# Attention turns in pairs of tiles: one burst of weighted sums for two tiles, small steps gathered, three output projections moved into the next turn

## The reference

```
h = relu(layernorm(x))                          # ahead of every phase
# l0: projected attention
q, k = h @ Wq.T, h @ Wk.T;  v = h @ Wv.T + bv
a = einsum('bnhd,bmhd->bhnm', q, k) * 384 ** -0.5 + adj
a = softmax(where(all(a == 0, -1), -inf, a));  a = nan_to_num(a)
x = x + einsum('bhnm,bmhd->bnhd', a, v) @ Wo.T + bo
# l3: plain attention, no output projection
scores = q @ k.T / sqrt(32) + beta * adj, masked where adj is 0
x = x + einsum('bhqk,bhkd->bhqd', softmax(scores), v)
```

## Time and profile before

| what | value |
|---|---|
| median of 3 runs | 2840.08 us (2840.01 to 2840.34) |
| profiled execution, own time | 2840.32 us |
| its span, first to last instruction | 2838.6 us |
| mean granted TensorE clock | 0.978 |
| PE busy | 2708.2 us, 95% of the span |
| PEld busy | 2345.1 us, 83% |
| DVE busy | 1802.0 us, 63% |
| ACT busy | 1256.7 us, 44% |
| POOL busy | 1093.8 us, 39% |

### The profile page before, as it was taken

The page is one execution under the profiler, slowest core; times in us unless marked ns, Lnnn a source line. Parts: engine busy times, 40 slices in busy tenths (PEclk is TensorE's granted clock), DMA queues, the critical chain, the costliest instruction groups (busy, mean ns, idle before and its releaser), DMA issues. The chain is left out here.

```text
span 2838.6 us, 75948 instructions
## 1 busy us (share of the span) xinstructions
PE 2708.2 (95%) x29582; PEld 2345.1 (83%) x29582; DVE 1802.0 (63%) x4227; ACT 1256.7 (44%) x2212; POOL 1093.8 (39%) x1081
## 2 busy tenths in 40 slices
PE   6999999986999999999958999999999978999998
PEld 5888888875888888888847888888888867888887
DVE  5777777764445545544546787787777765666565
ACT  3444444434443444444433334343343325565564
POOL 2333333342323322332232444443444443545455
PEclk9999999998999999999988999999999988999999
DMA  4222222214112112211121111111111112222221
GB/s 139 71 70 66 65 62 62 67 51 150 35 56 78 41 45 76 78 33 55 48 80 43 51 50 50 49 60 39 55 55 48 49 52 72 79 91 80 84 89 59
DMA packets 186659, 183.15 MB, mean 65 GB/s; under 512 B 79568, under 2 KB 186064, under 8 KB 186576
## 3 DMA queue, kind: packets, MB, share of 16 engines
q1 hardware_dynamic: 186576, 181.99, 20.9%
HBM read 131.61 MB, written 50.33 MB: 64 GB/s over the span
## 5 line engine op out<-in xcount | busy, mean ns | idle before, releaser
L52 PE MATMUL l_psW<-w_hi,l_hT_hi 128*128 128x384 f32 x1920 | 681.7, 355 | 2.0 <-DVE l_vX L573 2.0
L52 PE MATMUL l_psW<-w_hi,l_hT_lo 128*128 128x384 f32 x1920 | 647.6, 337 | 0.0
L52 PE MATMUL l_psW<-w_lo,l_hT_hi 128*128 128x384 f32 x1920 | 645.2, 336 | 0.0
L52 PE MATMUL l_psW<-l_hT_hi,w_hi 128*128 128x512 f32 (+1 forms) x1242 | 495.7, 399 | 12.1 <-ACT l_m L1252 3.7
L52 PE MATMUL l_psW<-l_hT_hi,w_lo 128*128 128x512 f32 (+1 forms) x1242 | 469.8, 378 | 0.0
L52 PE MATMUL l_psW<-l_hT_lo,w_hi 128*128 128x512 f32 (+1 forms) x1242 | 469.1, 378 | 0.0
L52 PEld LDWEIGHTS l_psW<-w_hi,l_hT_hi 128*128 128x128 f32 x1920 | 362.0, 189 | 38.5 <-issue 24.6
L52 PEld LDWEIGHTS l_psW<-w_lo,l_hT_hi 128*128 128x128 f32 x1920 | 362.6, 189 | 0.7
L52 PEld LDWEIGHTS l_psW<-w_hi,l_hT_lo 128*128 128x128 f32 x1920 | 361.4, 188 | 0.0
L52 PEld LDWEIGHTS l_psW<-l_hT_hi,w_hi 128*128 128x128 f32 x1242 | 236.0, 190 | 69.6 <-issue 22.1
L52 PEld LDWEIGHTS l_psW<-l_hT_hi,w_lo 128*128 128x128 f32 x1242 | 235.5, 190 | 44.8
(11 more groups left out here) (160 smaller groups left out, 5145.8 us busy)
## 6 DMA issues: line engine op xcount, KB each, us to landing
after_l<-l_xr SPq DMA_DIRECT2D x192, 192.0 KB, 1.9
l_xl<-after_l SPq DMA_DIRECT2D x47, 768.0 KB, 4.7
l_xr<-after_l SPq DMA_DIRECT2D x32, 768.0 KB, 4.5
l_xl<-in_x SPq DMA_DIRECT2D x16, 768.0 KB, 4.8
l_xr<-in_x SPq DMA_DIRECT2D x64, 192.0 KB, 2.4
l_xr<-after_l SPq DMA_DIRECT2D x64, 192.0 KB, 2.3
out_x<-l_xr SPq DMA_DIRECT2D x64, 192.0 KB, 1.9
l_adj<-in_adj SPq DMA_DIRECT2D x48, 128.0 KB, 2.4
```

What stands on the lines that cost most here:

```text
L52: last = nc.tensor.matmul(out, lhs[a](c), rhs[b](c), start=(m == 0), stop=(m == n - 1))
```

## The change

Two tiles are handled together in the last steps of attention.

- `weigh` runs both tiles of a pair in one burst of 96 recorded matmuls. Its result takes the place of the scores in psS, so that it waits until all four tiles' scores are read. eT holds two tiles.
- `row_output`, and in l0 `out_transposes` and `oT_parts`, handle a pair at a time: half as many instructions, each with twice the elements. In l0 o_rows holds all four tiles. In l3 it still holds one pair, and the second pair waits for `result` of the first (`y_set`).
- In l0 three projections of a group (Y1, Y2, Y3) run in the next turn instead of two, and `result` and the stores move with them. V2 moves from the end of a turn to the next turn's start, V0 of the next group ahead of the first burst. T01 of the group after next is done at the end of the turn, right behind the scores. The banks of q, k, v and y are dealt out anew.
- DVE's order in l0: V2 and V3 are taken out ahead of the biases of tiles 2 and 3, and the statistics stand between `least(3)` and the second `row_output`. POOL's `residual` steps stand behind the last `less_maximum`.
- At the start of l0 two values are made ahead of turn 0 and no longer three, with the third query product ahead of the second key product.

The core of the diff:

```
-    eT = sb("eT", [P, PAIRS, P])
+    eT = sb("eT", [P, 2, PAIRS, P])
...
-    S_end = 2 * S_cols
+    O_cols = 2 * KC * (HD + 1)
...
-    O_all = psS[:, :, S_end:S_end + KC * (HD + 1)].rearrange("p r (c d) -> p r c d", c=KC)
+    O_all = psS[:, :, 0:O_cols].rearrange("p r (c d) -> p r c d", c=2 * KC)
...
+    y_bank = (1, 0, 1, 0)
+    q_bank, k_bank, v_bank = ((0, 0, 1), (1, 0, 0), (1, 1, 1, 0)) if proj else ((0, 0, 0), (1, 1, 1), (0, 1, 0, 1))
...
+        def row_output(i, p):
+            pair = slice(2 * p, 2 * p + 2)
             if proj:
+                dve.wait_ge(mn_set, i * TILES + 2 * p + 2)
+                nc.vector.scalar_tensor_tensor(most[:], mn[:, pair, :], -1.0, mx[:, pair, :], ALU.mult, ALU.max)
+            elif not (isinstance(i, int) and i == 0 and p == 0):
+                dve.wait_ge(y_set, i * TILES + 2 * p)
+            dve.wait_ge(o_done, i * 2 + p + 1)
...
         def projected_turn(i, opening, ahead, further):          # DVE
...
             maximum(i, 1)
+            values(i, 2)
+            values(i, 3)
             add_bias(i, 2)
+            maximum(i, 2)
...
+            add_bias(i, 3)
+            maximum(i, 3)
             least(i, 0)
+            least(i, 1)
             row_output(i, 0)
+            if ahead:
+                values(i + 1, 0)
+            least(i, 2)
+            least(i, 3)
             if further:
                 statistics(i + 2)
+            row_output(i, 1)
+            oT_parts(i, 0)
             if further:
                 shifts(i + 2)
+            oT_parts(i, 1)
             if ahead:
                 values(i + 1, 1)
...
+        def weigh(i, p):
+            wait_apart(v_set, i * TILES + 2 * p + 2)
+            wait_apart(eT_set, i * TILES + 2 * p + 2)
+            for x in range(2):
+                for a in range(PAIRS):
...
+        def out_transposes(i, p):
+            pe.wait_ge(o_set, i * 2 + p + 1)
...
         def projected_turn(i, opening, ahead, further):          # PE
             n = i + 1
+            if not opening:
+                project(i - 1, 1)
...
+            if ahead:
+                pe.wait_ge(v_set, n * TILES + 1)
+                keys(n, 0)
+            wait_apart(o_set, i * 2 + 1)
+            weigh(i, 1)
+            out_transposes(i, 0)
             if ahead:
+                pe.wait_ge(q_set, n * KC + 1)
+                queries(n, 1)
+            pe.wait_ge(oT_set, i * 2 + 1)
+            out_transposes(i, 1)
...
                 scores(n, 0)
                 scores(n, 1)
+                if further:
+                    pe.wait_ge(oT_set, i * 2 + 2)
+                    transposes(n + 1, 0)
+                    transposes(n + 1, 1)
```

More of the change, by code:

```diff
@@ L254, in turn @@
                 if not opening:
-                    store(i - 1, 2, True)
-                    store(i - 1, 3, True)
+                    for t in (1, 2, 3):
+                        store(i - 1, t, True)
                 if ahead:
@@ L260, in turn @@
                 store(i, 0, ahead)
-                store(i, 1, ahead)
                 if not ahead:
-                    store(i, 2, False)
-                    store(i, 3, False)
+                    for t in (1, 2, 3):
+                        store(i, t, False)
             else:
@@ L304, in projected_turn @@
             if not opening:
+                result(i - 1, 1)
+            less_maximum(i, 1)
+            if not opening:
                 result(i - 1, 2)
-            less_maximum(i, 1)
-            residual(i, 0)
+            less_maximum(i, 2)
             if not opening:
                 result(i - 1, 3)
-            less_maximum(i, 2)
+            less_maximum(i, 3)
+            residual(i, 0)
             residual(i, 1)
-            less_maximum(i, 3)
             if further:
@@ L317, in projected_turn @@
             result(i, 0)
-            result(i, 1)
             if not ahead:
-                result(i, 2)
-                result(i, 3)
+                for t in (1, 2, 3):
+                    result(i, t)
         def plain_turn(i, opening, ahead, further):
@@ L328, in plain_turn @@
             residual(i, 1)
+            less_maximum(i, 3)
             result(i, 0)
-            less_maximum(i, 3)
+            result(i, 1)
             if further:
                 roots(i + 2)
-            result(i, 1)
             residual(i, 2)
@@ L441, in projected_turn @@
                 keys(i + 1, 2)
-            y_copy(i, 1, 0 if ahead else 1)
+            y_copy(i, 0)
             if not ahead:
-                y_copy(i, 2, 0)
-                y_copy(i, 3, 1)
+                for t in (1, 2, 3):
+                    y_copy(i, t)
         def plain_turn(i, opening, ahead, further):
@@ L464, in plain_turn @@
             exponentials(i, 3)
+            eT_copy(i, 3)
             if ahead:
@@ L574, in values @@
             ins.then_inc(v_set, 1)
-        def row_output(i, t):
+        def row_output(i, p):
+            pair = slice(2 * p, 2 * p + 2)
             if proj:
[L578 to L583, removed]
+                dve.wait_ge(mn_set, i * TILES + 2 * p + 2)
[3 more added lines that the diff above has]
+            dve.wait_ge(o_done, i * 2 + p + 1)
+            sums = rs[:].rearrange("p t (c r) -> p r (t c)", r=HPC)
             step.done(nc.vector.reciprocal(sums, O_all[:, :, :, HD]))
@@ L609, in _ @@
         if proj:
-            for t in range(TILES - 1):
-                values(0, t)
+            values(0, 0)
+            values(0, 1)
         else:
@@ L619, in _ @@
         before = step.n
-        step.per = 2 + TILES * 2 if proj else 2 + TILES + 1
+        step.per = 2 + 2 * 2 if proj else 2 + 2 + 1
         def projected_turn(i, opening, ahead, further):
             step.turn(i, before if ahead else before - 2)
-            if not opening:
-                values(i, 2)
             if ahead:
@@ L679, in plain_turn @@
                 queries(i + 1, 0)
-            row_output(i, 1)
+            row_output(i, 0)
             if further:
@@ L684, in plain_turn @@
                 queries(i + 1, 1)
-            row_output(i, 2)
             if further:
                 shifts(i + 2)
+            row_output(i, 1)
             if ahead:
                 queries(i + 1, 2)
-            row_output(i, 3)
-            if ahead:
                 add_bias(i + 1, 0)
@@ L751, in exp_transposes @@
             ins.then_inc(eT_done, 1)
[L753 to L763, removed]
-            ins.then_inc(o_done, 1)
@@ L766, in out_transposes @@
[L766 to L770, removed]
+        def weigh(i, p):
[3 more added lines that the diff above has]
+                for a in range(PAIRS):
+                    for b in range(2):
+                        c, r = divmod(2 * a + b, HPC)
+                        lo = (x * KC + c) * (HD + 1)
+                        keys_b = slice(NODES * b, NODES * (b + 1))
+                        for g in range(2):
+                            ins = nc.tensor.matmul(psS[NODES * g:NODES * (g + 1), r, lo:lo + HD + 1],
+                                                   eT[keys_b, x, a, NODES * g:NODES * (g + 1)], vX[keys_b, 2 * p + x, g, a],
+                                                   start=True, stop=True)
+            ins.then_inc(o_done, 1)
@@ L771, in out_transposes, with project @@
+        def out_transposes(i, p):
+            pe.wait_ge(o_set, i * 2 + p + 1)
+            for x in range(2):
+                for c in range(KC):
+                    ins = nc.tensor.transpose(psP[:, x, c * P:(c + 1) * P], o_rows[:, 2 * p + x, c * P:(c + 1) * P], ident[:])
             ins.then_inc(oT_done, 1)
-        def project(i, t, bank, transposed=None):
-            pe.wait_ge(oT_set, i * TILES + (t + 1 if transposed is None else transposed))
+        def project(i, t):
+            pe.wait_ge(oT_set, i * 2 + t // 2 + 1)
@@ L775, in project @@
             oT = tuple((lambda c, x=x: x[:, t, c, :]) for x in (oT_hi, oT_lo))
-            split_matmul(nc, psW[bank][:, 0:D], oT, w_cols(O, slice(0, D))).then_inc(y_done, 1)
+            split_matmul(nc, psW[y_bank[t]][:, 0:D], oT, w_cols(O, slice(0, D))).then_inc(y_done, 1)
         def projected_turn(i, opening, ahead, further):
             n = i + 1
[L780 to L783, removed]
+            if not opening:
+                project(i - 1, 1)
@@ L789, in projected_turn @@
             scores(i, 3)
-            pe.wait_ge(hT_set if ahead else oT_set, n * TILES + 2 if ahead else i * TILES)
+            if ahead:
+                pe.wait_ge(hT_set, n * TILES + 2)
+            else:
+                pe.wait_ge(oT_set, i * 2)
             exp_transposes(i, 0)
-            pe.wait_ge(v_set, i * TILES + 3)
-            values(i, 3)
+            if not opening:
+                pe.wait_ge(v_set, i * TILES + 3)
+                project(i - 1, 2)
+            pe.wait_ge(eT_set, i * TILES + 1)
             if ahead:
-                pe.wait_ge(eT_set, i * TILES + 1)
                 transposes(n, 2)
```

205 lines of the change are left out of this document (81 added, 124 removed).

## The result

The changed kernel takes 2833.03 us (median of 9 runs, 2830.84 to 2834.45) against 2840.01 (9 runs, 2838.30 to 2841.24): a ratio of 0.9975, with a 95% interval of 0.9965 to 0.9986. That is 7.0 us less; the forecast was 2836.3, 3.7 less. The profiled execution took 2832.26 us with a span of 2830.4, so the two profiles differ by 8.2 us of span, and those 8.2 can be split. A turn is measured from the start of one burst of scores of tiles 0 and 1 (S01) to the next, and the first stretch from the start of the span.

A forecast was written before the change was run, and what follows sets the result against it. PE's work, switches and waits were taken to bound each turn. Terms -4.5 - 1.3 - 0.6 - 0.2 + 2.9 = -3.7 us took the profiled 2840.32 to 2836.6, given as 2836.3 us; 8 in 10 range 2824 to 2844.

The forecast's parts named there:

- A: Both phases: the turns' savings are eaten by the next wait; 2831 to 2841 us, the forecast itself, chance 0.55.
- 0.2% line: Whole kernel: 0.2%, 5.7 us, can be told from no change; faster is below 2834.4 us, chance 0.38.
- Part 1: Both attention phases: joining bursts saves switches between kinds of matmul, 0.62 us a turn in l0, 0.71 in l3.
- Part 2: l0's middle: PE's wait for DVE's low parts of h before the first exponential transposes goes, 0.35 us a turn.
- Part 3: l0 turn: new waits at K0 and O23 return 0.85 us, E1 0.03; turn 37.23 us, 14 turns -1.3 us.
- bound without any collision: l0 turn: without the L587 collisions DVE's way is 11.2 us and hidden; turn 36.37 us, -13.3 us.
- Part 4: l3 turn: E1 loses W0 as cover and waits 0.7 us; turn 29.65 to 29.69 us, -0.2 us taken.
- Part 5: Phase ends: l0's start -4.5 us, l0's last turn -0.6, l3's last turn +2.9.
- B: l0 or l3: at least one forecast wait isn't there; l0 alone gives 2824 us, l3 alone 2827; chance 0.25.
- C: Loop's branch behind T01 in l0: it shows, 0.8 us a turn if bare, time 2847 us; chance 0.10.
- D: L587 in l0 waits through all POOL's adjoining steps, up to 2 us a turn, 2860 us; chance 0.04.

The follow-up runs named there:

- split burst: The changed kernel with l3's second-pair burst split around Q2 (W2 Q2 W3 K2): one run of 2841.18 us, l3 turn 30.11 us.
- reordered POOL: The changed kernel with POOL's root ahead of all four residual steps of l0: 2828.73 us, ratio 0.9959.
- l0 alone: The changed kernel with l3 built by the old function, only l0 in the new order: 2829.08 us, ratio 0.9960.

## Why the prediction was right or wrong

The mechanism was the forecast's: both phases save on switches and l0 loses its old wait, and what comes next gives it back, in l3 all of it, in l0 about half (0.45 of 0.97 us, where 0.85 was forecast). The time fell inside A's range, 3.3 us below the point. Direction and size came out on the better side of the 0.2% line, on which the forecast had put the smaller chance.

- **Part 1, switches.** Right. Pair burst 1.54 us, entry 0.10, exit 0.15, slow first matmul 0.11; the split burst gave 0.344 for one joining against 0.33.
- **Part 2.** Right: l0's old wait is gone from the list.
- **Part 3, what is late next in l0.** The failed step, and the one that carries the difference: "L587 falls into it and ends with it", it being the root. It falls into it and takes 0.18 us. O23 starts 11.98 us behind W01 and not 12.3 (312.24 to 324.22), and the waits sum to 0.45, not 0.85. The layout also had a slip of the other sign: from 5.1 to 6.8 it leaves 1.7 for two minima of 0.94, which end at 6.9 (319.14), so without it the error would have been larger. With the measured waits the sum of Part 3 is 37.32 - 0.62 - 0.35 + 0.48 = 36.83 against 36.86 measured; 14 turns carry 5.2 us of error. The other collision, with the residual step, and K0's 0.2 were as forecast. I had priced the root by its length in the earlier trace rows, whose steps move 384 elements; no row of before showed L587 beside a root. The reordered POOL (36.47) came within 0.10 of the bound without any collision, 36.37; 0.04 of it is what O23 still waits.
- **Part 4, l3.** Right. E1 waits 0.39 and the k product 0.12, with restarts 0.67, forecast 0.7. The turn is 29.69, top of 29.65 to 29.69. With the cover given back the turn fell to 29.33, which shows that it is the missing burst in front of E1.
- **Part 5, the ends.** l0's start gave 4.0 of 4.5 us. Its waits are 3.0, 0.9 and 0.3 us, 4.2 for 4.0, and the granted clock over the window of the earlier trace rows rose from 0.74 to 0.87. l3's end came out at +2.9 as forecast, but by luck, since its parts did not: from the last burst's start to the end it is 9.4 us for 5.9 (+3.5, forecast 2.7), and the turn ahead of that burst was 0.6 shorter (forecast 0.2 longer).
- **Rivals.** B, a wait that isn't there, is half true: one of three collisions did not happen. C is out: the last transpose of T01 and Y1 behind it start 0.03 us apart, as transposes and products do elsewhere in the turn. D is out: L589 ended with the first of two adjoining residual steps, the second going on for another 1 us. (Its 2860 is low: 2 us in 14 turns on top of 2836.3 make 2864.)

The profiles differ by 8.2 us and the medians by 7.0, and each profile is one execution. What scatters most between executions are the stretches in which PE idles and its granted clock falls. The last turn of l0, the same code, took 34.6 us in the profile of the changed kernel, 36.9 in four of the profiles after it and 33.7 in the three with the reordered POOL, with a granted clock of 0.99 (the 2.4 GHz level; the changed kernel) and of 0.53 (nearly the 1.2 GHz level; l0 alone) in the same stretch. In the 8 us ahead of it PE was busy for 5.6 and 5.4 us.

```profile
616.00:624.00 8.00, 6.11 (x38) 5.97 (x38) 2.15 (x3) 2.92 (x5) 2.02 (x2) 0.99 0.08 26
```

```profile
616.00:624.00 8.00, 6.16 (x23) 6.16 (x24) 1.97 (x3) 2.10 (x3) 1.00 (x1) 0.53 0.00 0
```

The first row is the changed kernel, the second l0 alone. So the -1.2 of that row in the table is one draw from a spread of about 3 us, and the ends can't be forecast to better than that. What sets the moment at which the clock falls there was not tried. The 0.4 us between the phases was not followed up.

## What to carry to other kernels

Joining bursts is worth its switches, here 0.33 us each, only where the work taken from between hides nothing: in l3 the single burst in front of E1 was the cover of a chain, and one joining and one split were better than two joinings. When a small VectorE instruction with two SBUF inputs sits on the path, look at what GpSimd runs beside it, and move GpSimd's wide steps behind it; that was one line and 4 to 5 us. Price a collision by a row with the same pair of instructions, or keep both ends: duration alone misled.

## What the runs showed of the hardware

- A VectorE product of 24 elements a partition with two SBUF inputs ends with the GpSimd addition of 384 elements that runs when it begins (0.68 us in the changed kernel, 0.77 with a residual step in the root's place), but takes its 0.18 us beside a GpSimd power of 4 elements that the profile shows as 1.02 us long. Instructions with an input in PSUM (the reciprocal 0.31, the scaled rows 0.96) and the minimum with one SBUF input (0.94) took the same time whatever GpSimd ran.
- The page SBUF — State Buffer of the Trainium skill says, under Who interferes with whom, that a VectorE instruction with two SBUF inputs contends with a GpSimd instruction that reads SBUF, and, under Summary: rules for kernel authors, that the second of the two to issue is blocked until the first finishes. The additions agree with it (0.18 grows to 0.68). The root reads SBUF too, and by the rule the second L589 would have ended with it at 322.71, 0.48 us later than it did. The measurement differs there: what counts isn't the step's length in the profile. Whether the root reads its few elements and then computes, no run here shows.
- A wait shorter than the modelled tail of a matmul isn't in the list of waits: 0.45 us a turn of l0 (0.20 at K0, 0.25 at O23) stood in the distances between starts alone.
